# Fixed semaphore lanes for some DMAs of a three-stage transformer layer on eight cores

## The reference, cut to what matters

```python
x = x + 0.5 * ffn(layernorm(x))      # "MoE" block: one shared expert, 8 experts, top-2, trunc(prob)
x = x + attn_block(layernorm(x))     # attention, 16 heads, distance bias, + LN, FFN 1024-4096-1024, + LN
x = x + 0.5 * ffn(layernorm(x))      # the same MoE block again

# ffn:        (relu(x@Ws1)**2)@Ws2 + sum_e prob_e * (relu(x@W1[e])**2)@W2[e]
# attn_block: x1 = LN(t + softmax(q k^T - dist)/.. v @ Wo + bo)*g1 + be1
#             z  = LN(relu(x1@W1+b1)@W2+b2 + x1)*g2 + be2
```

## Time and profile before

| what | value |
|---|---|
| median of 3 runs | 3748.51 us (3745.41 to 3751.84) |
| profiled execution, its own time | 3747.4 us |
| its span on the slowest core (core 3) | 3745.9 us |
| spans of the eight cores | 3728.1 to 3745.9 us |
| TensorE busy | 2623.5 us, 70% of the span |
| VectorE busy | 1540.6 us, 41% |
| ScalarE busy | 1042.1 us, 28% |
| GpSimd (POOL) busy | 222.8 us, 6% |
| DMA moved | 204.21 MB in 226665 packets |

### The profile page before, as it was taken

The page is one execution under the profiler, slowest core; times in us unless marked ns, Lnnn a source line. Parts: engine busy times, 40 slices in busy tenths (PEclk is TensorE's granted clock), DMA queues, the critical chain, the costliest instruction groups (busy, mean ns, idle before and its releaser), DMA issues.

```text
span 3745.9 us, 34205 instructions; the slowest of 8 cores (3728.1 to 3745.9 us)
## 1 busy us (share of the span) xinstructions
PE 2623.5 (70%) x10819; PEld 1011.4 (27%) x10819; DVE 1540.6 (41%) x3256; ACT 1042.1 (28%) x1322; POOL 222.8 (6%) x117
## 2 busy tenths in 40 slices
PE   4319999954966666656666683958668521999997
PEld 2114444422421111111111131423223101444443
DVE  3543444452045555555555373011120254344445
ACT  0201111121335555555555413121212210111110
POOL 0200000012000000000000043010100130000000
PEclk9659999977977777777777695979889755999996
DMA  3031322123899800000000020625445301111002
GB/s 91 0 52 34 57 36 44 29 90 72 97 111 113 107 1 1 1 0 1 1 1 1 23 90 13 150 85 118 129 85 144 64 0 45 40 57 52 28 29 90
DMA packets 226665, 204.21 MB, mean 55 GB/s; under 512 B 148199, under 2 KB 199528, under 8 KB 223224
## 3 DMA queue, kind: packets, MB, share of 16 engines
q1 hardware_dynamic: 205996, 139.10, 13.7%
q0 software_dynamic: 20496, 62.93, 13.4%
HBM read 248.09 MB, written 52.51 MB: 80 GB/s over the span
## 4 chain that ended last, share of the span: by engine, by line
PE 58%; DVE 17%; ACT 10%; issue 7%; DMA 4%; POOL 2%; DVEq 1%; SPq 0%; ACTq 0%; POOLq 0%
PE pA L432 13%; PE pB L475 13%; PE pA L873 6%; PE pB L904 5%; ACT AR L669 5%; PE pB L644 5%; DVE AR L676 4%; PE pA L707 3%; PE pA L523 3%; PE pA L660 2%; PE pB L556 1%; DVE AR L288 1%; DVE AR L699 1%; DVE AR L711 1%; POOL AR L282 1%
## 5 line engine op out<-in xcount | busy, mean ns | idle before, releaser
L432 PE MATMUL pA<-AR 128*128 128x512 bf16 x2304 | 503.0, 381 | 7.9 <-DMA AR<-wcWs 7.9
L475 PE MATMUL pB<-AR 128*128 128x512 bf16 x2304 | 499.2, 379 | 0.3 <-DVE AR L456 0.3
L676 DVE TENSOR_TENSOR AR<-AR 128x512 bf16<-128x512 bf16 x1024 | 384.7, 418 | 244.7 <-ACT AR L669 223.3
L644 PE MATMUL pB<-AR 128*65 128x512 bf16 x1024 | 354.1, 431 | 162.9 <-DVE AR L686 83.7
L669 ACT ACTIVATE AR<-pA 128x1024 bf16<-128x1024 f32 x352 | 350.9, 1023 | 238.4 <-PE pA L660 236.7
L444 ACT ACTIVATE AR<-pA 128x512 bf16<-128x512 f32 x288 | 156.3, 595 | 803.1 <-PE pA L432 803.1
L873 PE MATMUL pA<-AR 128*128 128x512 bf16 x1024 | 230.8, 389 | 147.6 <-DMA AR<-wcW1a 96.8
L483 DVE SCALAR_TENSOR_TENSOR AR<-pB,AR 128x512 f32<-128x512 f32 x320 | 220.4, 691 | 260.2 <-PE pB L475 260.1
L432 PEld LDWEIGHTS pA<-AR 128*128 128x128 bf16 x2304 | 226.3, 98 | 282.7 <-issue 13.5
L475 PEld LDWEIGHTS pB<-AR 128*128 128x128 bf16 x2304 | 225.3, 98 | 272.6 <-issue 1.3
L707 PE MATMUL pA<-AR,onesrs 1*64 1x512 f32 x128 | 113.3, 982 | 204.5 <-ACT AR L704 204.5
(11 more groups left out here) (134 smaller groups left out, 2040.8 us busy)
## 6 DMA issues: line engine op xcount, KB each, us to landing
AR<-wcW1a SPq DMA_DIRECT2D x32, 1024.0 KB, 5.2
AR<-wcW2a SPq DMA_DIRECT2D x32, 1024.0 KB, 6.7
AR<-x SPq DMA_DIRECT2D x16, 512.0 KB, 3.7
AR<-W1e POOLq DMA_DIRECT2D x8, 1024.0 KB, 16.7
AR<-W2e POOLq DMA_DIRECT2D x8, 1024.0 KB, 12.9
AR<-probsp SPq DMA_DIRECT2D x16, 512.0 KB, 11.9
x1sp<-AR SPq DMA_DIRECT2D x8, 1024.0 KB, 4.3
wcW1a<-W1a POOLq DMA_DIRECT2D x1, 8192.0 KB, 94.1
```

The costliest lines, as they stand in the source:

```text
L432: lastmm = p.on("tensor", lambda e, j=j, dc=dc, fc=fc, tq=tq, ps=pp[f2]: e.matmul(ps, w1v[j][:, dc, 128 * fc:128 * (fc + 1)], xn(dc)[:, 51 ...
L475: lastmm = p.on("tensor", lambda e, j=j, fc=fc, do=do, tq=tq, ps=ps: e.matmul(ps, w2v[j][:, fc, 128 * do:128 * (do + 1)], h2s(j, fc, tq), ...
L644: last = p.on("tensor", lambda e, uc=uc, hh=hh, h=h: e.matmul(accs[hh][0:65, :], self.av_slice(uc, h), ptb[uc % 3][:, 512 * hh:512 * (hh + ...
L676: tv = p.on("vector", lambda e, sl=sl, off=off, hh=hh: e.tensor_tensor(ptb[sl][:, 512 * hh:512 * (hh + 1)], ebuf[sl][:, 512 * hh:512 * (hh ...
```

## The change

`dma()` gets an optional argument `lane`. A DMA that gives it takes that semaphore and doesn't advance the counter that deals out the others; the wait for the DMA before it on its lane stays. It is used for `bq` and the eight parameter vectors (SP lane 7), the two `rowsp` stores and the two `rowsp` loads (SP lane 5), the eight `x1sp` stores (SP lane 6) and the six weight copies (POOL lane 3). What is loaded, stored and computed, and the order in which each engine issues its DMAs, stay as they are.

```diff
-    def dma(self, eng, out, in_, wait=(), slow=False):
+    def dma(self, eng, out, in_, wait=(), slow=False, lane=None):
         base = DMA_SEM[eng]
         nl = self.DMA_LANES[eng]
-        idx = self.dma_idx.get(eng, 0)
-        self.dma_idx[eng] = idx + 1
-        lane = "%s%d" % (base, idx % nl)
+        if lane is None:
+            idx = self.dma_idx.get(eng, 0)
+            self.dma_idx[eng] = idx + 1
+            lane = "%s%d" % (base, idx % nl)
+        else:
+            lane = "%s%d" % (base, lane % nl)
         prev = self.ctr.get(lane, 0)
         w = list(wait) + ([(lane, prev)] if prev else [])
...
-            tok_sp_mu = p.dma("sync", self.rowsp_d[:, 0:T], row, wait=[t2])
+            tok_sp_mu = p.dma("sync", self.rowsp_d[:, 0:T], row, wait=[t2],
+                              lane=5)
...
-            tok_sp_r = p.dma("sync", self.rowsp_d[:, T:2 * T], row, wait=[t7])
+            tok_sp_r = p.dma("sync", self.rowsp_d[:, T:2 * T], row, wait=[t7],
+                              lane=5)
...
             trr = p.dma("sync", row, self.rowsp_d[:, T * i:T * (i + 1)],
-                        wait=[self.tok_attn_A] + (tok_tiles[-4:] if i else []))
+                        wait=[self.tok_attn_A] + (tok_tiles[-4:] if i else []),
+                        lane=5)
...
         self.tok_bq = self.dma(
             "sync", self.bq8c, self.bq_d.rearrange("o (c p) -> p (o c)", p=128),
-            slow=True)
+            slow=True, lane=7)
...
             tpc = self.dma("sync", pc[:, dst_lo:dst_lo + w_],
-                           src.rearrange("o (c p) -> p (o c)", p=128), slow=True)
+                           src.rearrange("o (c p) -> p (o c)", p=128), slow=True,
+                           lane=7)
...
                                self.xr[:, 2048 * dc:2048 * (dc + 1)],
-                               wait=[tok_moe_tq[dc]])
+                               wait=[tok_moe_tq[dc]], lane=6)
...
-                self.tok_wc_ffn = self.dma("gpsimd", dst, src)
+                self.tok_wc_ffn = self.dma("gpsimd", dst, src, lane=3)
...
-                self.tok_wc_moe = self.dma("gpsimd", dst, src)
+                self.tok_wc_moe = self.dma("gpsimd", dst, src, lane=3)
```

## The result

The changed kernel takes 3763.7 us in the median of 14 runs, against 3750.3 us for the kernel before in 14 runs. The ratio is 1.0033, with a 95% interval from 1.0023 to 1.0042: some 12 us, or a third of a percent, slower. A number of runs of both kernels fell into a state in which one die is granted a lower clock; they are left out of every ratio here, which is why some medians stand above what their ratio says.

The account below looks back on a forecast made before the run. It took TensorE's matmul chain, begun by the first sequence load, to bound the kernel; the vectors' row delays that load 24.6 us, all else nothing: 3748.5 + 24.6 = 3773 us, range 3761 to 3784 us.

Parts of the forecast that it names:

- The start is on the path, one for one: At the kernel's start, TensorE's first matmul waits for the first sequence load; any delay reaches the end in full, 24.6 us.
- The nine vectors wait one at a time, and the first sequence load stands behind them: In SP's queue at the start, each vector after bq waits for a full landing; be2's issue moves from 17.20 to 41.8 us.
- The term 7 x 4.4 + 8.3 = 39.1 us: Loads ahead of be2 at the start: seven vectors at 4.4 us, b1a at 8.3; with 2.70 us, be2 issued at 41.8.
- three rows that "agreed within 0.2 us": Profile readings for b2a (4.4 us), Wr (4.2) and be2 (4.3), same element count, taken as one vector load's 4.4 us.
- Its own sign of being wrong: Wrong if vectors under 3 us apart, first matmul to end differing over about 10 us, or new DMA waits at L523/L781.
- The range: For 8 in 10: 3.1 to 5.6 us a vector, b1a 7.7 to 8.7, +15 to +33 us: 3761 to 3784 us.
- the wide bounds: Outer limits on be2's issue at the start: 1.9 to 6.0 us a vector, +2.9 to +36.4 us.
- Rival 1, the round trip alone: At the start, a lone vector lands in 1.9 to 2.7 us; start moves 3 to 8 us, 3751 to 3756; 7 in 100.
- the forecast's thin end: Lower part of the forecast for the vectors at the start: 2.9 us a vector, 10 us more in time.
- Rival 2, the clock: Over the whole kernel, TensorE's granted clock rises by 0.007 and pays the delay back; 3740 us; 4 in 100.
- The stores, 4.3 to 4.9 us each, done by 854 us with 13 to 17 us of slack: Before the Q projection, the eight x1sp stores one at a time end before Wq's issue at 866.94 us; cost nothing.
- The weight copies: POOL's six copies one at a time add 2 to 4 us each; Wo lands by some 1330 us, 800 us of cover.

Follow-up runs that it names:

- x5: The changed kernel, but POOL's load of Wr waits until the parameter vectors have landed; one time, 3759.0 us.
- x7: The changed kernel, but the eight x1sp stores are 32 of 256 KB, one at a time on lane 6; one run, 3777.0 us.
- x8: The changed kernel, but the eight x1sp stores are 64 of 128 KB, one at a time on lane 6; 3816.5 us.

## Why the prediction was right, and where its size was off

- *The start is on the path, one for one.* Right, and shown in both directions: with the vectors in a row the end comes later, and with the vectors moved away it comes earlier. In the means over the cores it is +10.6 us at the first matmul, +9.6 at the Q projection and +10.9 at the end of the span. That the slowest cores have 12.6 us at be2 and 12.7 at the first matmul, so near the 12 us of the ratio, is partly chance: they are core 3 and core 1, and on one and the same core the first matmul moved by 8 to 14 us.
- *The nine vectors wait one at a time, and the first sequence load stands behind them.* Right, row by row.
- *The term 7 x 4.4 + 8.3 = 39.1 us.* This is the step that was mis-sized; it measured 29.81 - 2.70 = 27.1 us. b1a was 6.35 against 8.3 and bq 4.29 against 4.4, but the other six were 2.69 to 2.87 against 4.4: 10 of the 12 us between forecast and result. The three rows that "agreed within 0.2 us" measured other things: b2a had b1a's elements and g1's around it, be2 had g2's, and Wr goes by POOL's queue. For Wr bq isn't the reason: with bq out of the way (x5, where the first sequence loads were beside it instead) it took 4.3 us in the mean over the cores, against 4.5 in the changed kernel. For b2a and be2 no run takes the excess apart; for bq, 1.0 us went away with Wr. Their agreement was chance and said nothing of a load from SP that has nothing else in flight. The interpolation that the rows allowed, between identf with 128 runs at 1.9 us and b1a's packets at 4.1 us for 4096 elements, would have been nearer: some 1 us per 1024 elements on top of 1.9 us puts be2 at 2.70 + 7 x 2.9 + 6.0 = 29.0 us, and it was issued at 29.81.
- *Its own sign of being wrong.* The prediction calls itself wrong if the vectors are under 3 us apart, and six of them are 2.69 to 2.87 us apart; it wanted be2 near 42 us and the first matmul near 49, and they came at 29.81 and 37.12. By that sign its price failed. The two other signs didn't come: from the first matmul to the end the two profiled executions differ by 3 us, and no new wait on a DMA stands at L523 or L781 (now L528 and L787).
- *The range.* The time lies in it, 3763.7 us against 3761 to 3784, by luck. The range began at 3.1 us a vector and +15 us, and the measured 2.7 us and +12 us are both below that. It is the 2 us allowed for the medians that let it in, and the median that stands above its ratio: 3748.5 us times 1.0033 would have been 3760.9. Only the wide bounds, 1.9 to 6.0 us a vector, held the value.
- *Rival 1, the round trip alone.* Its mechanism isn't so: there is 1.5 us of round trip and 1.2 us per 1024 elements. Its price was nearer than the forecast's all the same: it had 1.9 to 2.7 us a vector, the forecast's thin end 2.9, and the six measured fall between the two. Its time, 3 to 8 us, fell short by bq and b1a. The Trainium skill (DMA: Bandwidth & Descriptors, Anatomy of one DMA) states about 2.0 us and bytes at 436 GB/s, for the software path and with the generation of descriptors small; as an estimate from it a vector would be 2.0 us and b1a 2.04. The six plain vectors took 2.7 us, 0.7 us more, and b1a 6.35, so for loads of single elements the measurement decides against it.
- *Rival 2, the clock.* The profiled executions have nearly the same granted clock on the two dies (medians of their cores), 0.817 and 0.819 before, 0.818 and 0.818 after, and the mean span rose as much as the first matmul was late; there is no sign that anything was paid back.
- *The stores, 4.3 to 4.9 us each, done by 854 us with 13 to 17 us of slack.* 3.9 us each, over some 31 us after the first one's issue; right. The price that x7's expectation gave for the end of the cover was too low: a large load that overlaps the row makes each of its waits longer.
- *The weight copies.* Wo's issue was forecast near 1300 us and came at 1292.72. Right, with no cost.

One difference between the profiles is the clock's and not the kernels'. From the first store of the router's result to the first rowsp store, the first MoE block with its normalization's sums, the mean over the cores was 521.5 us before and 521.3 in the changed kernel, but 523.8 without the vectors' lane, 523.6 and 524.8 with the vectors' lane only, and 523.9 to 524.8 in three kernels with the input early. Late and early starts are both among them, so the start isn't the reason. Core by core the stretch takes 521 to 522 us on some cores and up to 527 on others of the same execution, often the four cores of one die. Here are two cores of the run without the vectors' lane, from 420 to 560 us; the number before the last two is TensorE's granted clock, and the first count is that of its matmuls:

```profile
420.00:560.00 140.00, 140.00 (x644) 63.15 (x643) 61.26 (x127) 23.87 (x44) 5.04 (x6) 0.99 0.29 47
```

```profile
420.00:560.00 140.00, 140.00 (x650) 63.47 (x649) 61.79 (x127) 23.88 (x44) 5.03 (x6) 1.00 0.31 47
```

The first is core 1, with 526.7 us for the stretch, the second core 5, with 521.1. TensorE is busy throughout on both, and 1% of the clock is 1% of the matmuls and 5 us of the stretch. The kernels x5 to x8, which ran in one batch, have 521.3 to 521.4 us. Why the clock stood at 0.99 on these cores stays open.

## What to carry to other kernels

Waiting for each DMA before issuing the next costs a round trip per DMA, and that costs time only where something that the path needs is queued behind the row. So look first at what stands behind the waits on the issuing engine, then at their number; putting small loads that are needed late behind the first loads that are needed at once was worth more here (17 us) than any choice of semaphores tried (12 us between the dealt and the fixed ones). To price a DMA alone from a trace in which all of them overlap, fit a fixed part and a part per element over loads of different sizes, rather than averaging loads of one size that have others beside them, and without taking a DMA of another queue for it.

## What was not expected of the hardware

- In a row, 1 MB, 256 KB and 128 KB stores landed in 3.9, 2.1 and 1.7 us (medians). The differences, 2.2 us for 896 KB, are about 417 GB/s, and leave about 1.4 us for a DMA without its bytes.
- Single 4-byte elements, 1024 to a vector, cost about 1.2 us per 1024 in a row on the slowest core, and 1.0 in the mean over the cores of the same kernel.
- A 256 KB store beside POOL's two 2 MB weight loads took up to 8.9 us, four times its usual 2.1.
- The same queue is not the same on every core: the first sequence load of the changed kernel was issued between 26.90 and 30.23 us, and its first matmul started between 31.35 and 37.12 us.
